# Flamingo block on one core: evictions between context chunks, gate products spread, last row transposes issued by SyncE

## The reference, cut to what matters

```python
x = x + tanh(g_xattn[0]) * quant_matmul(layernorm(x), ctx)          # 8-bit fake quantisation of both
x = x + tanh(g_ffn[0])   * lora_ffn(layernorm(x))                   # x @ W_org.T + 8 mixed LoRA experts
x = x + tanh(g_xattn[1]) * attention(layernorm(x), ctx, ctx)        # 32 query heads, 8 key/value heads
x = x + tanh(g_ffn[1])   * moe(layernorm(x))
# moe: gate = softmax([h, ratio] @ gate_w + gate_b), ratio = mean|h| of the text rows / of the vision rows
#      the two experts of a batch are those of its first row; out = sum of share * expert(h)
#      expert = act(h @ w1 + b1) @ w2 + b2, act one of tanh, gelu, silu
```

## Time and profile before

| | us |
|---|---|
| median of the runs | 1250.55 |
| profiled execution | 1254.74 |
| its span, first to last instruction | 1252.90 |
| PE busy in the span | 1223.0 |
| DVE busy | 822.5 |
| POOL busy | 681.5 |
| ACT busy | 476.8 |

### The profile page before, as it was taken

How to read it: one execution, slowest core, us unless ns; L and a number is a source line. 1 busy time by engine, 2 the same in 40 slices (tenths; PEclk the granted TensorE clock), 3 DMA queues, 4 the chain that set the end, 5 groups by cost and what they waited for, 6 DMA issues and landing times.

```text
span 1252.9 us, 16926 instructions
## 1 busy us (share of the span) xinstructions
PE 1223.0 (98%) x6504; PEld 511.6 (41%) x6504; DVE 822.5 (66%) x1417; ACT 476.8 (38%) x826; POOL 681.5 (54%) x300
## 2 busy tenths in 40 slices
PE   8998899999999899999999999999989999999998
PEld 6664444444444232222222222234444444444443
DVE  7997833433356789989999899345528855737622
ACT  4675411000100467767777677743352010010000
POOL 6006997400043578888988898860263453624510
PEclk9998999999999999999999999999989999999999
DMA  9576243311532254545445454533493442523301
GB/s 353 170 250 168 85 130 106 68 34 35 115 110 76 60 120 106 116 92 108 108 102 117 91 117 87 101 69 59 133 213 97 138 121 100 183 84 101 117 16 51
DMA packets 86764, 141.20 MB, mean 113 GB/s; under 512 B 49056, under 2 KB 59296, under 8 KB 82592
## 3 DMA queue, kind: packets, MB, share of 16 engines
q1 hardware_dynamic: 45840, 94.03, 24.0%
q0 software_dynamic: 4608, 33.56, 13.3%
q10 hardware_dynamic: 36240, 12.60, 5.1%
HBM read 85.49 MB, written 10.49 MB: 77 GB/s over the span
## 4 chain that ended last, share of the span: by engine, by line
PE 76%; DVE 16%; DMA 2%; issue 2%; POOL 2%; ACT 1%; ACTq 0%; SPq 0%; POOLq 0%; DVEq 0%
PE bank L642 46%; PE bank L892 9%; DVE mxp L1625 8%; PE bank L879 6%; PE bank L961 5%; PE bank L924 5%; DVE xn L1615 2%; PE bank L678 2%; PE bank L668 1%; DVE R L1406 1%; DMA stage_c<-w_in 1%; DVE R L1359 1%; DMA R<-R 1%; POOL R L608 1%; POOL R L630 1%
## 5 line engine op out<-in xcount | busy, mean ns | idle before, releaser
L1625 DVE TENSOR_REDUCE mxp<-bank 128x1 f32<-128x512 f32 x512 | 320.2, 679 | 60.7 <-PE bank L879 60.4
L1275 ACT ACTIVATE R<-bank 128x512 f32<-128x512 f32 x512 | 273.9, 602 | 116.5 <-PE bank L961 113.3
L642 PE MATMUL bank<-XTh,R 128*128 128x512 bf16 x896 | 280.7, 383 | 4.6 <-POOL R L630 4.4
L608 POOL TENSOR_TENSOR R<-R 128x2048 f32<-128x2048 f32 x48 | 218.6, 4555 | 35.5 <-ACT R L1275 29.4
L642 PE MATMUL bank<-R 128*128 128x512 bf16 x960 | 209.2, 379 | 0.0
L642 PE MATMUL bank<-XTl,R 128*128 128x512 bf16 x448 | 171.5, 383 | 0.0
L630 POOL TENSOR_TENSOR R<-stage_pair,R 128x1024 bf16<-128x1024 f32 x32 | 75.4, 2371 | 140.4 <-DVE R L1779 85.8
L642 PEld LDWEIGHTS bank<-R 128*128 128x128 bf16 x960 | 93.7, 98 | 113.5
L879 PE MATMUL bank<-R 96*128 96x512 bf16 x352 | 134.8, 383 | 4.6 <-DVE mxp L1625 3.0
L892 PE MATMUL bank<-R,stage_c 128*32 128x512 f32 x1024 | 137.3, 608 | 0.5 <-ACT R L1275 0.5
L961 PE MATMUL bank<-R 98*128 98x512 bf16 x352 | 134.5, 382 | 2.0 <-ACT R L1275 2.0
(11 more groups left out here) (194 smaller groups left out, 1489.0 us busy)
## 6 DMA issues: line engine op xcount, KB each, us to landing
stage_pair<-wts_in SPq DMA_DIRECT2D x35, 512.0 KB, 3.6
R<-R POOLq DMA_DIRECT2D x16, 1024.0 KB, 7.0
stage_pair<-R POOLq DMA_DIRECT2D x16, 1024.0 KB, 7.0
stage_pair<-w_in SPq DMA_DIRECT2D x32, 512.0 KB, 3.6
stage_c<-w_in SPq DMA_DIRECT2D x32, 512.0 KB, 3.7
R<-q_scr SPq DMA_DIRECT2D x48, 128.0 KB, 2.5
XTh<-ctx_t_in SPq DMA_DIRECT2D x11, 512.0 KB, 7.4
XTh<-ctx_nat_in SPq DMA_DIRECT2D x9, 512.0 KB, 3.6
```

What stands on the lines that cost most here:

```text
L608: pool.tensor_tensor(PS[(0, 1, 2, 1)[j]], PB[2 * j % 4], PB[2 * j % 4 + 1], ALU.add).then_inc(p_add, 1)
L642: mm = pe.matmul(o, a, m, start=first and a is ah and bs is bh, stop=last and a is al)
L1275: act.activation(PB[kt % 4][:, h * S:(h + 1) * S], bank[t_bank(g, t)][:, :], ACT.Exp, scale=float(HD) ** -0.5).then_inc(exp_done, 1)
L1625: dve.tensor_reduce(mxp[head // REP % 2][:, m, n // 2, n % 2:n % 2 + 1], bank[s_bank(u)][:, :], AX.X, ALU.max).then_inc(s_max, 1)
```

## The change

Nothing is computed differently, except that the gate's upper and lower weights lie side by side (gwb), so that a row chunk's upper part is multiplied by both in one matmul of 6 columns, and DVE adds the two results: 64 matmuls a batch instead of 96. The rest is order. (a) `values_out(1)` and `keys_out(1)` stand earlier among the context chunks on DVE and ACT, `column_sums(1)` comes after `quantised_tile(3)` on PE. (b) SP loads an "o" chunk at each of the first eight query items; TensorE's attention starts when 14 queries are out, and its first two steps wait for the last two. (c) The gate matmuls of batch 0 stand one by one behind the matmuls of output tiles 5 and 6, those of batch 1 between the first layer's. (d) SP, not ACT, issues the transposes of row tiles 5, 6 and 7, between its loads of w1. (e) ACT's upper parts of w1 come earlier between the rows, those of w2 one behind each activation. (f) DVE adds tile 5's output to X before it chooses the experts. (g) The last two chunks of the first layer are taken bank by bank.

```diff
@@ -159,8 +159,7 @@
-        gwh = sb("gwh", [P, KT * EXPERTS], BF16)
-        gwl = sb("gwl", [P, KT * EXPERTS], BF16)
+        gwb = sb("gwb", [P, KT * 2 * EXPERTS], BF16)
...
@@ -453,8 +452,8 @@
                 if item == Q_TURN:
                     rows_in(0)
                 queries_out(b, c)
-                if c % 2 == 1:
-                    load_weights(WT_AT["o"] + item // 2, 1)
+                if item < KT:
+                    load_weights(WT_AT["o"] + item, 1)
                 if item < Q_KEYS:
                     sp.wait_ge(q_out[c], 16 * 2)
                     queries_in(item)
@@ -485,8 +484,27 @@
             sp.wait_ge(wt_done, N_WT)
             sp.wait_ge(o_lo, GROUPS)
             sp.wait_ge(st_mm, STEPS * GROUPS)
+
+            def turn_upper(t):
+                sp.wait_ge(nat_hi, TT + t + 1)
+                sp.dma_start_transpose(out=per_tile(XTh)[:, :, t * P:(t + 1) * P], in_=nat_h).then_inc(hi_t[t], 16)
+
+            def turn_lower(t):
+                sp.wait_ge(nat_lo, TT + t + 1)
+                sp.dma_start_transpose(out=per_tile(XTl)[:, :, t * P:(t + 1) * P], in_=nat_l).then_inc(lo_t[t], 16)
+
             e = expert(0)
-            load_expert(W1_N(0), w1, e, 0, KT)
+            load_expert(W1_N(0), w1, e, 0, RING_E)
+            sp.wait_ge(hi_t[TT - 4], 32)
+            sp.wait_ge(lo_t[TT - 4], 32)
+            turn_upper(TT - 3)
+            turn_lower(TT - 3)
+            load_expert(W1_N(0), w1, e, RING_E, RING_E + 1)
+            turn_upper(TT - 2)
+            load_expert(W1_N(0), w1, e, RING_E + 1, KT)
+            turn_lower(TT - 2)
+            turn_upper(TT - 1)
+            turn_lower(TT - 1)
@@ -769,12 +787,12 @@
             pe.wait_ge(k_lo, 8)
             for t in range(2):
                 quantised_tile(t)
-            pe.wait_ge(c_done, len(CHUNKS))
-            column_sums(1)
             quantised_tile(2)
             pe.wait_ge(cb_done, 2)
             turn_behind(0, 0)
             quantised_tile(3)
+            pe.wait_ge(c_done, len(CHUNKS))
+            column_sums(1)
             turn_behind(1, 1)
@@ -925,12 +943,16 @@
                                    start=k == 0 and i == 0, stop=k == KT - 1 and i == 2)
                 return mm
 
-            def output_tile(t):
+            def output_tile(t, gate_parts=range(0)):
 
                 pe.wait_ge(x_up, 2 * (2 * TT + t - 1))
                 for k in range(KT):
-                    mm = output_part(t, k, 0, 6)
-                mm.then_inc(nat_mm, 1)
+                    for n in range(6):
+                        mm = output_part(t, k, n, n + 1)
+                        if k == KT - 1 and n == 5:
+                            mm.then_inc(nat_mm, 1)
+                        if 6 * k + n < len(gate_parts):
+                            gate_part(0, gate_parts[6 * k + n])
@@ -956,6 +978,8 @@
                     turning = g + 1 < GROUPS and t > TURN_AT
                     if turning and t == TURN_AT + 3:
                         pe.wait_ge(row_lo, g + 2)
+                    elif STEPS * g + t < 2:
+                        pe.wait_ge(q_lo, B * KT - 1 + t)
-            pe.wait_ge(q_lo, B * KT)
+            pe.wait_ge(q_lo, B * KT - 2)
+            def gate_part(b, n):
+
+                t, k, low = b * TB + n // (2 * KT), n // 2 % KT, n % 2
+                if n % (2 * KT) == 0:
+                    rows_in_place(2, range(t, t + 1))
+                if n == 0:
+                    pe.wait_ge(rt_read, b)
+                cols = slice(k * D + t * P, k * D + (t + 1) * P)
+                count = EXPERTS if low else 2 * EXPERTS
+                mm = pe.matmul(bank[6][:, 2 * t * EXPERTS:2 * t * EXPERTS + count], (XTl if low else XTh)[:, cols],
+                               gwb[:, 2 * k * EXPERTS:2 * k * EXPERTS + count], start=k == 0 and not low,
+                               stop=k == KT - 1 and low == 1, skip_group_check=True)
+                if n == 2 * KT * TB - 1:
+                    mm.then_inc(lg_mm, 1)
+                    pe.wait_ge(am_done, 4 * (b + 1))
+                    pe.matmul(bank[7][:, b * 2 * TB:(b + 1) * 2 * TB], onesf[:, :],
+                              AM[:, b, :, :].rearrange("p a t -> p (a t)"), start=True, stop=True).then_inc(as_mm, 1)
-            for t in range(TB, TT - 2):
-                output_tile(t)
-            gate_logits(0)
-            for t in range(TT - 2, TT):
-                output_tile(t)
+            output_tile(TB)
+            output_tile(TB + 1, range(0, 48))
+            output_tile(TB + 2, range(48, 64))
+            output_tile(TB + 3)
-            for k in range(KT):
+            def first_part(f, k):
+
+                if k == 0 and f % 2 == 0:
+                    pe.wait_ge(x_up, 6 * TT - 2 + f)
+                w = slice(k * D + f * P, k * D + (f + 1) * P)
+                mm = triple([bank[f][:, :]], w1_h[:, w], w1_l[:, w], [XTh[:, k * D:k * D + S]],
+                            [XTl[:, k * D:k * D + S]], k == 0, k == KT - 1)
+                if k == KT - 1:
+                    mm.then_inc(a_mm, 1)
+
...
+            for k in range(KT - 2):
                 pe.wait_ge(wt_done, W1_N(0) + k + 1)
                 for f in range(4):
+                    first_part(f, k)
+                    if k < 4:
+                        gate_part(1, 8 * k + 2 * f)
+                        gate_part(1, 8 * k + 2 * f + 1)
+            pe.wait_ge(wt_done, W1_N(0) + KT)
+            for f in range(4):
+                for k in range(KT - 2, KT):
+                    first_part(f, k)
+                    gate_part(1, 32 + 4 * f + 2 * (k - KT + 2))
+                    gate_part(1, 33 + 4 * f + 2 * (k - KT + 2))
+            for n in range(48, 64):
+                gate_part(1, n)
-            chunks(26, 31)
+            chunks(26, 29)
             values_out(1)
-            chunks(31, 32)
+            chunks(29, 30)
             keys_out(1)
+            chunks(30, 32)
...
@@ -1309,15 +1356,30 @@
                     act.activation((w1_h, w2_h)[c // KT][:, ds(c % KT, D)], stage_e[c % RING_E][:, :],
                                    ACT.Copy).then_inc(ew_act, 1)
 
+            divided_hi(GROUPS - 1)
             for t in range(TT - 3):
-                if t == 0:
-                    divided_hi(GROUPS - 1)
-                rows_turned(2 * TT + t, t, rooted=t == 0)
+                if t > 0:
+                    root(3 * TT + t, t % 2)
+                    turn_lower(2 * TT + t - 1, t - 1)
+                rows_upper(2 * TT + t, t)
+                turn_upper(2 * TT + t, t)
+                absolute_sum(t)
+            root(4 * TT - 3, 1)
+            turn_lower(3 * TT - 4, TT - 4)
             act.wait_ge(pv_mm, KT * GROUPS)
             act.wait_ge(p_add, KT // 2 * GROUPS)
-            for t, before, after in ((TT - 3, (0, 2), (2, 2)), (TT - 2, (4, 2), (6, 1)), (TT - 1, (7, 1), (8, 4))):
-                rows_turned(2 * TT + t, t, before_lower=lambda before=before: weights_hi(*before))
-                weights_hi(*after)
+            rows_upper(3 * TT - 3, TT - 3)
+            absolute_sum(TT - 3)
+            root(4 * TT - 2, 0)
+            weights_hi(0, 2)
+            rows_upper(3 * TT - 2, TT - 2)
+            absolute_sum(TT - 2)
+            weights_hi(2, 2)
+            root(4 * TT - 1, 1)
+            weights_hi(4, 2)
+            rows_upper(3 * TT - 1, TT - 1)
+            absolute_sum(TT - 1)
+            weights_hi(6, 2)
-                            if s == 0 and f == KT // 2 - 1:
-                                weights_hi(12, 4)
+                            if s == 0:
+                                weights_hi(KT + f, 1)
             x_step(7)
             chunks(20, 23)
             quantise_x(7)
-            chunks(23, 31)
+            chunks(23, 27)
+            values_out(1)
+            chunks(27, 28)
+            keys_out(1)
             dve.wait_ge(rowq_done, TT)
             dve.tensor_scalar(rterm[:, :], rowq[:, :], qc[:, 5:6], qc[:, 4:5], ALU.add, ALU.mult).then_inc(rterm_done, 1)
-            values_out(1)
-            chunks(31, 32)
-            keys_out(1)
+            chunks(28, 30)
@@ -1552,12 +1617,13 @@
 
             dve.wait_ge(k_out, 32)
             column_terms(0)
+            chunks(30, 32)
             quantised_update(0)
             quantised_update(1)
-            column_terms(1)
             for t in range(TT):
                 dve.wait_ge(xq_t[t], 16)
             quantised_update(2)
+            column_terms(1)
             for t in range(3, TT - 1):
-                nxt(dve.tensor_tensor(L[:, tiles, :],
-                                      bank[6][:, b * TB * EXPERTS:(b + 1) * TB * EXPERTS].rearrange("p (t e) -> p t e", e=EXPERTS),
-                                      rb[:, b:b + 1, :].to_broadcast([P, TB, EXPERTS]), ALU.add))
+                logits = bank[6][:, 2 * b * TB * EXPERTS:2 * (b + 1) * TB * EXPERTS].rearrange("p (t i e) -> p i t e", i=2, e=EXPERTS)
```

(8 more changed lines are left out.)

49 lines of the change are left out of this document (17 added, 32 removed).

## The result

The changed kernel took 1244.5 us (median of five runs, 1244.43 to 1244.74) against 1250.55 of the kernel before (median of five as well, 1250.0 to 1256.23). The ratio, taken from all the runs and not from the two medians (whose quotient is 0.9952), is 0.9939, 95% interval 0.9916 to 0.9962. The forecast was 1232 with a range of 1229 to 1241: the sign was right, but two thirds of the gain did not come. The profiled execution took 1244.74 us with a span of 1242.9; before 1254.74. So 10.0 us went from one profile to the other, where the sum had 18.5.

A forecast was written before the change was run, and what follows sets the result against it. TensorE was taken as the bound, busy 1223.0 of 1252.9 us. Gains of 4.4 + 4.0 + 10.1 = 18.5 us took the profiled 1254.7 to 1236.2, median 1232, range 1229 to 1241.

The forecast's parts named there:

- the sum: Gains forecast over the whole kernel, 4.4 + 4.0 + 10.1 = 18.5 us off the profiled 1254.7.
- Bounds of the kernel: Whole kernel: TensorE bounds it; 1440 matmuls run without a gap from 937.15, so a microsecond won earlier counts fully.
- A: End of the context: DVE's first update at 103.0 instead of 107.45, worth 4.4 us, at worst 2.
- two chunks 2.7, 98.9; column terms 1.4, 100.3; ... two chunks 2.7, 103.0: End of the context, DVE's schedule: last two chunks in 2.7 us beside POOL's first addition, first update at 103.0.
- B: Start of the attention: POOL's first addition starts 3.2 us earlier, ACT's 2.00 us wait goes; 4.0 us, bounds 0 and 5.0.
- C: Output tile 5 to hidden tile 4: less PE work and no PE waits, worth 10.1 us, lower bound 1.
- I follow it by the old durations: Output rows to first expert, ACT's new order: last lower part of w1 at about 920.5, 2 us before PE needs it.
- (1): SP's queue: transposes and loads hold each other up, pass 7 waits 2 to 6 us; 1242.3 us profiled, chance 0.15.
- (2): Gate matmuls between large ones cost a whole weight load, 0.098 us, 8.7 us more PE; 1245.0 profiled, chance 0.08.
- (3): Context end or attention start: gain given back to transposes, POOL or ACT, 4 us lost; 1240.2 profiled, chance 0.10.
- (4): Transposes on SP's queue take 10 to 13 us, making the kernel slower; 1257.9 us profiled, chance 0.03.
- From the profile to the median: Whole kernel: profiled execution lay 4.2 us over the median 1250.55, so 1236.2 profiled became a median of 1232.

The follow-up runs named there:

- the repaired kernels: Changed kernel with POOL's first addition held until DVE's last chunk (1241.48 us), both last chunks ahead of the column terms (1241.31), or only one ahead (1240.56).
- experiment 5: Kernel before with only the middle part: output-weight loads at the first eight query items, wait for the last two queries moved into the first score steps; 1248.81 us.
- experiment 6: Kernel before with only the last part: gate products spread, SP issuing the transposes, expert weights split one by one; 1247.55 us.
- experiment 7: Changed kernel with both last chunks ahead of the column terms, plus only two loads of w1, not four, before row 4's lower transpose; 1238.51 us.
- 10: Changed kernel with both last chunks ahead of the column terms, plus batch 0's gates in one block behind output tile 5, batch 1's still spread; 1238.38 us.
- experiment 4: Changed kernel with the end of the context put back as in the kernel before, the other two parts kept; 1242.75 us.

## Why the prediction was wrong, step by step

**Bounds of the kernel.** Right: every microsecond ahead of 937 was won or lost for the whole; the last 1440 matmuls went at the same pace.

**A: wrong, and the failed step is "two chunks 2.7, 98.9; column terms 1.4, 100.3; ... two chunks 2.7, 103.0".** The change puts DVE's last two chunks beside POOL's first additions, and the step costed them as if POOL stood still, even counting it as a saving that POOL's 2.53 us "now lies beside these two chunks". They took 100.09 to 108.96, 8.9 us for 2.7. The slot had nothing to give in the other order either: the column terms end at 100.2, two chunks are 2.7 us and POOL's first addition 2.5, one after the other 105.4, and the repaired kernels have their first update at 105.42, 105.25 and, with half a chunk got in ahead of POOL, 104.90, not at 103.0. Of the rest of A, what the traces show held: the sums at 92.6 in 3.62 us, the transposes no bound (0.44 us of wait). The bounds of A, 2 and 4.4, had no room for the -1.85 that came, so the range was too narrow on this side. The trace of before held the sign, in rows that I had not compared: the same DVE instruction with POOL idle and with POOL working beside it (last row).

```profile
896.03 0.81 DVE L1692 TENSOR_SCALAR xn<-X,mv,lnv 128x1024 f32<-128x1024 f32 x1
...
920.76 1.68 DVE L1692 TENSOR_SCALAR xn<-X,mv,lnv 128x1024 f32<-128x1024 f32 x1
```

```profile
919.77 2.13 POOL L630 TENSOR_TENSOR R<-stage_c,R 128x1024 bf16<-128x1024 f32 x1 [4.25 <-ACT R L1309]
```

**B: right.** 4.0 forecast, 4.3 by the trace, 4.1 by experiment 5. The slow clock in its sum (1.1 us of it and a part of 0.5) is lost in some executions and not in all, as the profile of experiment 6 shows. POOL's first addition starts 1.6 us earlier on the clock (426.08 for 427.68), in a stage that part A had made 1.85 us later: together 3.45 against the 3.2 us forecast.

**C: the sum of PE's work right, the waits missed, the size off by 2.5.** Of the 58.75 us from output tile 5 to hidden tile 4, 56.3 were forecast; the three waits add 2.67 and the cheaper gates take 0.6 off, which leaves 0.4 without an account. The failed step is "I follow it by the old durations". The step looked for the hold-up on SP's queue and found the last lower part 2 us early. It missed that the four loads go out just ahead of ACT's last transpose (7.6 us instead of some 3), and that the spread gates, 3.2 us later than in a block, hold up DVE, whose row work stands behind the choice of experts. Experiments 7 and 10 remove one of these each, and each gives the 2.7 us back (2.8 and 2.9 by the medians). DVE's row instructions also lie beside POOL's again (1.68 us instead of 0.81), which no experiment took away; in 7 and 10 the same instruction takes 1.68 to 1.93 us and PE waits for nothing.

**Rivals.** (1), transposes and loads holding each other on SP's queue: a loss of 2.5 us where it had 6, and in another place. SP's own transposes took 3.0 to 3.6 us; only the lower one of row tile 6, behind two loads, took 4.4, and one behind two loads in experiment 7 took 5.7. That fits the rule that the prediction cites from the Trainium skill (DMA: Bandwidth & Descriptors, section Queues, rings and completion order), but PE waited for none of these transposes. What PE did wait for hung on the one transpose of ACT's and on the late choice of experts. (2), a gate matmul at 0.098 us: refuted, 0.025; the weight load is hidden between large matmuls that use all rows. The rule cited for this rival from the Trainium skill (TensorE: Matmul & The Clock Gate, section The mechanism) does not hold here. (3), A or B given back: this happened to A, and more than all of it, by a mechanism that the rival did not name. (4), 10 to 13 us a transpose on SP: refuted, 4.4 at most. (Its sum also added 4 us for a stretch of slow clock that the earlier trace rows price at 1.7; the range did not hang on it.)

**From the profile to the median: wrong by 4 us.** The forecast took off 4.2 us because the profiled execution of before lay that far over its median. But the kernel before scatters (1249.9 to 1256.2 us, mean clock 0.992 to 0.995 in the last runs), and the changed one does not (1244.43 to 1244.74, clock 0.997). The slower executions have the lower clock, so what put that profile above the median was mostly lost clock, and the sum had already counted its stretches of slow clock as won; taking 4.2 us off counted them a second time. That the clock was lost behind the waits of B and C is likely and not shown, as no trace of another execution of before was kept: with only A's wait of 5.0 us left as it was (experiment 4) the runs spread over 0.9 us, with C's left as well (5) or B's (6) over 3.2 and 3.8. The 1250.55 itself was also a low draw; beside the experiments the same kernel had 1251.7 to 1253.1. Of the 12.5 us between forecast and result, 6.2 are A, 2.5 are C, -0.3 is B and about 4 are this.

## What to carry to other kernels

Before work is moved into the shade of a wait, look at who is busy there: DVE's fast instructions on SBUF and POOL's additions do not run beside each other, so such a slot is no cover for DVE (8.9 us for 2.7 here). When a result is made later, even by 2 us, list what stands behind its consumer in that engine's order. And if one profiled execution lies above the median, the excess is part of what the change may remove, and is not to be taken off again.
